# A fused attention and expert kernel: the first group of each attention program gets a PSUM bank for each of its four projections, and the value blocks are cleared behind the first moments

## What is computed

```python
x = x + L0_attention(layernorm(x), context)              # 16 heads of 8, no mask
x = x + L0_ffn(layernorm(x))                             # 8 experts pick 8 tokens each, attend, scatter back
# L1: three residual steps inside one block
x = x + L1_block(layernorm(x), context, mask_q, mask_k)  # self attention, cross attention, feed-forward of 512
x = x + L1_moe(layernorm(x))                             # 16 routed experts, 4 chosen, and 2 shared ones

def attention(xq, xkv, Wq, bq, Wk, bk, Wv, bv, Wo, bo, mask):
    q, k, v = xq @ Wq + bq, xkv @ Wk + bk, xkv @ Wv + bv
    scores = q @ k.T / sqrt(8)                           # per head
    return softmax(masked(scores)) @ v @ Wo + bo
```

## Time and profile before

| | |
|---|---|
| median of 3 runs | 2140.08 us (2134.15 to 2143.28) |
| time of the profiled execution | 2129.31 us |
| its span in the profile | 2127.5 us |
| TensorE busy | 1974.6 us, 93% |
| VectorE busy | 1629.4 us, 77% |
| ScalarE busy | 1063.6 us, 50% |
| GpSimd busy | 465.4 us, 22% |
| DMA over the span | 14 GB/s |
| granted TensorE clock, mean | 0.979 |
| first attention program | 0 to about 334 us |
| choice of tokens | about 334 to 591 us |
| second attention program | about 591 to 1295 us |
| late part | about 1295 us to the end |

### The profile page before, as it was taken

The page is one execution under the profiler, slowest core; times in us unless marked ns, Lnnn a source line. Parts: engine busy times, 40 slices in busy tenths (PEclk is TensorE's granted clock), DMA queues, the critical chain, the costliest instruction groups (busy, mean ns, idle before and its releaser), DMA issues. The chain is left out here.

```text
span 2127.5 us, 52756 instructions
## 1 busy us (share of the span) xinstructions
PE 1974.6 (93%) x19220; PEld 1530.4 (72%) x19220; DVE 1629.4 (77%) x4569; ACT 1063.6 (50%) x2180; POOL 465.4 (22%) x520
## 2 busy tenths in 40 slices
PE   7999995888869999999999998989999999999998
PEld 4666673677736666666666665767888888888887
DVE  5777775777538888888888884678888878888886
ACT  5656652666625555555455443544444444444442
POOL 1111111111002232323223223762111211111111
PEclk9999997999969999999999998999999999999999
DMA  3000000000000000001000002000000000000000
GB/s 128 31 30 20 30 10 1 1 1 1 1 20 2 0 0 0 0 1 32 20 30 30 20 10 68 1 1 6 6 6 5 10 6 5 6 6 10 6 5 11
DMA packets 27409, 30.50 MB, mean 14 GB/s; under 512 B 1952, under 2 KB 20640, under 8 KB 27040
## 3 DMA queue, kind: packets, MB, share of 16 engines
q1 hardware_dynamic: 27296, 29.18, 4.2%
HBM read 24.98 MB, written 4.19 MB: 14 GB/s over the span
## 5 line engine op out<-in xcount | busy, mean ns | idle before, releaser
L491 DVE TENSOR_REDUCE mx<-ps 128x8 f32<-128x512 f32 x384 | 261.9, 682 | 162.7 <-PE ps L681 162.5
L398 ACT ACTIVATE ex<-ps 128x512 f32<-128x512 f32 x384 | 230.2, 600 | 259.1 <-PE ps L699 257.0
L1125 ACT ACTIVATE y_res<-ps 128x512 f32<-128x512 f32 x288 | 172.4, 599 | 355.4 <-PE ps L1211 355.3
L1193 PEld LDWEIGHTS ps<-down,y_res 128*128 128x128 f32 x2048 | 267.2, 191 | 25.0 <-issue 3.0
L699 PE MATMUL ps<-pack,sh 128*128 128x128 f32 x1536 | 249.5, 284 | 29.7 <-DVE sh L493 28.8
L493 DVE TENSOR_TENSOR sh<-ps,mx 128x512 f32<-128x512 f32 x384 | 265.4, 691 | 13.2
L1193 PE MATMUL ps<-down,y_res 128*128 128x128 f32 x2048 | 270.7, 275 | 1.4 <-DVE y_res L1479 1.4
L1461 DVE TENSOR_TENSOR y_res<-ps,y_res 128x512 f32<-128x512 f32 x288 | 197.6, 686 | 80.4 <-PE ps L1211 66.0
L715 PEld LDWEIGHTS ps<-vblk,ex 128*64 128x64 f32 x6144 | 211.5, 138 | 65.0 <-issue 65.0
L699 PEld LDWEIGHTS ps<-pack,sh 128*128 128x128 f32 x1536 | 168.1, 141 | 121.2 <-issue 62.2
L715 PE MATMUL ps<-vblk,ex 128*64 128x32 f32 x6144 | 254.4, 226 | 0.0
(11 more groups left out here) (237 smaller groups left out, 3388.6 us busy)
## 6 DMA issues: line engine op xcount, KB each, us to landing
ctxT<-in_ctx SPq DMA_DIRECT2D x32, 256.0 KB, 2.8
x_res<-in_x SPq DMA_DIRECT2D x16, 256.0 KB, 2.8
kmi<-in_key_mask SPq DMA_DIRECT2D x16, 256.0 KB, 3.3
out<-y_res SPq DMA_DIRECT2D x16, 256.0 KB, 2.3
pack<-in_pack SPq DMA_DIRECT2D x1, 2053.0 KB, 10.2
wqkv<-in_wqkv SPq DMA_DIRECT2D x1, 1536.0 KB, 10.8
gate<-in_gate SPq DMA_DIRECT2D x6, 192.0 KB, 3.6
up<-in_up SPq DMA_DIRECT2D x6, 192.0 KB, 3.8
```

What stands on the lines that cost most here:

```text
L398: nc.scalar.activation(ex[:, u % 2], UB[u % 4].rearrange("p (c n) -> p c n", n=P), ACT.Exp).then_inc(e_ready, 1)
L491: nc.vector.tensor_reduce(mx[:, u % 2], sc, AX.X, ALU.max).then_inc(max_done, 1)
L1193: last = nc.tensor.matmul(YB[k % 2][:, t * D:(t + 1) * D], act_[:, k % 3, t * P:(t + 1) * P], down[:, k, :], start=True, stop=True)
```

## The change

It does three things. First, in the start of each attention program the rounds go to different banks: xT to `PREP`, k, q and v to the score banks `UB[0]`, `UB[1]` and `UB[2]`, which no one uses yet. TensorE then waits in the start only for the copy of xT (which q needs, and for a = 1 also k and v), no longer for the round before. Since `scores` of units 2 and 3 write `UB[2]`, TensorE waits there, in the first group, for all four copies. Second, in the second attention program VectorE takes the first moments ahead of the three memsets; in the first program the memsets stay where they were. ScalarE waits for the memsets only ahead of its first `copy_v`. Third, since q may now be copied by VectorE while k's copies run on ScalarE, the first q counts in a semaphore of its own, `first_q_copied`; ScalarE waits for it after k's copies and counts it on in `prep_copied`.

```diff
+        FIRST_BANK = {"xT": PREP, "k": UB[0], "q": UB[1], "v": UB[2]}
...
                     elif r == "k":
                         for j in range(HQ):
-                            spread_key(L, g, s, j)
+                            spread_key(L, g, s, j, FIRST_BANK[r])
                     elif r == "q":
                         if L.a == 0:
-                            copy_q(L, g, s)
+                            copy_q(L, g, s, FIRST_BANK[r])
                     else:
-                        copy_v(L, g, s)
+                        if L.a != 0:
+
+                            act.wait_ge(first_q_copied, 1)
+                            act.sem_inc(prep_copied, 1)
+                        act.wait_ge(vblk_set, 3)
+                        copy_v(L, g, s, FIRST_BANK[r])
...
-            act.wait_ge(vblk_set, 3)
             if a == 0:
                 act.wait_ge(consts_set, 3)
...
             def prep(g, s, L):
                 norm_stats(L, g, s)
                 key_mask_of_next(L, g, s)
-                copy_q(L, g, s)
+                if L.a != 0:
+                    clear_values()
+                copy_q(L, g, s, FIRST_BANK["q"], first_q_copied)
...
-                if n > 0:
+                bank = FIRST_BANK[what] if start else PREP
+                if start:
+                    if n > L.nr("xT"):
+                        pe.wait_ge(prep_copied, L.nr("xT") + 1)
+                elif n > 0:
                     pe.wait_ge(prep_copied, nth(g, NP, n - 1))
-                elif not start:
+                else:
                     pe.wait_ge(prep_copied, g * NP)
...
             def free_banks(g, u, first):
+                if first and u == 2:
+
+                    pe.wait_ge(prep_copied, NP)
```

More of the change, by code:

```diff
@@ L359, in copy_xT, with spread_key @@
                 nc.scalar.copy(srcT[:, :], PREP).then_inc(prep_copied, 1)
-            def spread_key(L, g, s, j):
+            def spread_key(L, g, s, j, bank=PREP):
                 if j == 0:
                     act.wait_ge(prep_ready, nth(g, NP, L.nr("k")))
-                last = nc.scalar.activation(kblk[:, s, :, j, :], by_batch(PREP), ACT.Identity, bias=L.bkm[:, j:j + 1],
+                last = nc.scalar.activation(kblk[:, s, :, j, :], by_batch(bank), ACT.Identity, bias=L.bkm[:, j:j + 1],
                                             scale=headmask[:, j:j + 1])
@@ L368, in spread_key, with copy_q, copy_v @@
                     last.then_inc(prep_copied, 1)
-            def copy_q(L, g, s):
+            def copy_q(L, g, s, bank=PREP):
                 act.wait_ge(prep_ready, nth(g, NP, L.nr("q")))
-                nc.scalar.activation(qd[:, s], PREP, ACT.Identity, bias=C["bqs"], scale=SCALE).then_inc(prep_copied, 1)
-            def copy_v(L, g, s):
+                nc.scalar.activation(qd[:, s], bank, ACT.Identity, bias=C["bqs"], scale=SCALE).then_inc(prep_copied, 1)
+            def copy_v(L, g, s, bank=PREP):
                 act.wait_ge(prep_ready, nth(g, NP, L.nr("v")))
@@ L381, in copy_v @@
                                 "p (t b) r e -> p b t r e", b=2)[:, b],
-                            PREP[64 * b:64 * b + 64, :].rearrange("p (t r j e) -> p j t r e", t=TILES, j=2, e=DH)[:, j])
+                            bank[64 * b:64 * b + 64, :].rearrange("p (t r j e) -> p j t r e", t=TILES, j=2, e=DH)[:, j])
                 last.then_inc(prep_copied, 1)
@@ L473, in key_mask_of_next, with copy_q @@
                                         ).then_inc(kmask_ready, 1)
-            def copy_q(L, g, s):
+            def copy_q(L, g, s, bank=PREP, copied=prep_copied):
                 if L.a == 0:
@@ L484, in copy_q @@
                     sc = qsc[:, s].unsqueeze(2).broadcast_to((P, GB, S))
-                nc.vector.scalar_tensor_tensor(by_batch(qd[:, s]), by_batch(PREP), L.bq, sc, ALU.add, ALU.mult
-                                               ).then_inc(prep_copied, 1)
+                nc.vector.scalar_tensor_tensor(by_batch(qd[:, s]), by_batch(bank), L.bq, sc, ALU.add, ALU.mult
+                                               ).then_inc(copied, 1)
             def shift(g, u):
@@ L573, in later_constants, with clear_values @@
                                             setup["any"][:, 2 + f:3 + f], None, ALU.mult).then_inc(qscale_diag, 1)
+            def clear_values():
+                nc.vector.memset(vblk[:, :, :, :, :], 0.0).then_inc(vblk_set, 1)
+                dve.wait_ge(vblk_set, 1)
+                nc.vector.memset(vblk[0:64, :, :, :, DH:DH + 1], 1.0).then_inc(vblk_set, 1)
+                nc.vector.memset(vblk[64:128, :, :, :, 16 + DH:17 + DH], 1.0).then_inc(vblk_set, 1)
             def prep(g, s, L):
@@ L641, in prep_slot @@
                     for t in range(TILES):
-                        last = nc.tensor.transpose(PREP[:, t * P:(t + 1) * P], xn[:, s, t, :], ident)
+                        last = nc.tensor.transpose(bank[:, t * P:(t + 1) * P], xn[:, s, t, :], ident)
                 elif what == "k":
@@ L645, in prep_slot @@
                         pe.wait_ge(c_loaded[s], loaded(L, g, s))
-                    last = nc.tensor.matmul(PREP, L.wk, source(L, s), start=True, stop=True)
+                    last = nc.tensor.matmul(bank, L.wk, source(L, s), start=True, stop=True)
                 elif what == "q":
-                    last = nc.tensor.matmul(PREP, L.wq, srcT[:, :], start=True, stop=True)
+                    last = nc.tensor.matmul(bank, L.wq, srcT[:, :], start=True, stop=True)
                 else:
                     for t in range(TILES):
-                        last = nc.tensor.matmul(PREP[:, t * D:(t + 1) * D], source(L, s)[:, t * P:(t + 1) * P], L.wv,
+                        last = nc.tensor.matmul(bank[:, t * D:(t + 1) * D], source(L, s)[:, t * P:(t + 1) * P], L.wv,
                                                 start=True, stop=True)
```

1 line of the change is left out of this document (added).

## The result

| | before | after |
|---|---|---|
| median | 2134.15 us (2129.23 to 2143.49, 15 runs) | 2127.27 us (2118.19 to 2132.79, 15 runs) |
| ratio | | 0.9958, 95% interval 0.9938 to 0.9977 |
| profiled execution, span | 2129.31 us, 2127.5 us | 2131.81 us, 2130.0 us |

The change is 0.42% faster, 9.0 us of 2134.15, with an interval of 4.9 to 13.2 us. The ratio is formed from all the runs; the two medians alone lie 6.9 us apart. More runs of the kernel before have moved its own median from the 2140.08 of the three shown first to 2134.15. The profiled execution after the change is 2.5 us *longer* than the one of before. A reader who compares just these two profiles would call the change a loss, so the first question is where in that profile the time was won and where it was lost.

A forecast was written before the change was run, and what follows sets the result against it. The prediction took the two serial program starts, where nothing hides the four rounds, as what counts: 7.12 us from the second plus 0.98 from the first, 8.1 us off 2140.1, gives 2132.0 us; range 2122 to 2139.

The forecast's parts named there:

- Moments ahead of the clearing: Second program's start: the moments, and the chain to q's matmul, come 4.16 us earlier, with the clearing hidden beside them.
- k behind q: Second program's start: k's matmul waits for xT's copy alone and follows q's matmul directly, 1.05 us gained.
- Scores behind k's copies: Second program's start: scores no longer wait behind v's matmul, 2.01 us gone, less 0.10 for passing on q's copy.
- First program, 0.98: First program's start: v's matmul comes right behind q's, and v and the scores move 0.98 us earlier.
- The clock, second start: Second program's start: early rise given back within the first pair, lasting rise as late as before, counted from the scores.
- The first rival: Clock rises early and stays, or returns a pair or two earlier: 7.4 us more gain, 2124.6 us; chance 0.31.
- The clock, first start: First program's start: q and v back to back for about 4 us may also bring the early clock; within the 0.31 rival.
- the third rival: Either start: a later clock rise pays back part, one pair more at half clock costing 3.5 us, 2135.5; chance 0.11.
- GpSimd held by the clearing: Second program's start: reciprocal waits for the memset's end, all behind it 3.4 us later, gain 4.7, 2135.4; chance 0.07.
- Slower: First groups: the clock stays down longer; two groups more would cost 28 us, 2160; chance 0.03.
- doesn't do what it says: Starts: another wait keeps k behind q or scores behind v, leaving only 4.16 us, 2135.9; chance 0.01.

The follow-up runs named there:

- the order alone: Kernel before, one bank kept, with only the moments moved in front of the clearing in the second program; ratio 0.9969 (0.9953 to 0.9985).
- the banks alone: Changed kernel, four banks kept, with the clearing back in front of the moments in both programs; ratio 0.9986 (0.9972 to 1.0).
- keeping the clock up: Changed kernel plus seven matmuls whose result no one reads in the second program's start; ratio to the kernel before 0.9922 (0.9900 to 0.9944).
- the memset in halves: Changed kernel with the big memset cut into two of 2048 elements; timed once, 2128.90 us.
- the clearing three times: Changed kernel with the big memset done three times in the second program; timed once, 2130.71 us.

## Why the prediction was right

The forecast was a gain of 8.1 us, 0.38%, within half a per cent; measured were 9.0 us, 0.42%. The absolute time is 4.7 us under the 2132.0 named, because the median it was taken from stood 5.9 us too high, and the two medians differ by 6.9 us and not by 8.1. The interval of 4.9 to 13.2 us doesn't tell 8.1 from 9.0, nor from the 9.6 that the starts add up to in this profile, so that the total came so close is in part luck. By its own steps:

- *Moments ahead of the clearing, 4.16.* Measured 5.05: by the first DMA issue the moments began at 5.09 before and at 0.04 now. The term was mis-sized. The 4.16 went from the memset's recorded start, and its first 0.80 us stood hidden in the 1.84 us of idle behind the barrier (0.95 now). The halves show that these 0.8 belong to the memset. The prediction had taken the 3.47 alone as its cost, and with it 0.85 ns an element, where the two together are 1.04. The Trainium skill ("VectorE: DVE Perf Modes", Zero memsets can be issued as uint32) gives a memset one cycle per element, and its Specifications give VectorE 0.96 GHz. An estimate from these is 4.27 us for 4096 elements, and the trace agrees: 0.80 + 3.47.
- *k behind q, 1.05.* 1.86 us from q to k where 1.87 was taken.
- *Scores behind k's copies.* From k's matmul to the first copy 1.88 us, not 2.11: the clock had risen just before. From the first copy to the scores 2.93, the 2.84 and 0.09 for the passing on, put at 0.10.
- Together 8.3 in place of 7.12 for the second start.
- *First program, 0.98.* 1.28 in this profile from q's matmul to the scores, since v ran into the full clock. Whether anything of it reaches the end depends on the clock (below).
- *The clock, second start.* It rose early and fell within the first pair, as forecast, and the lasting rise kept its distance of about 21 us to the first scores. The reason given for the fall is not shown. The prediction read the fall at 1285 to 1286 as one under small matmuls, with TensorE busy for all of that microsecond; the row just ahead (1283.76) stands behind 1.30 us of idle time, and this fall behind 2.08. Nothing here separates the small matmuls from the idle time. And of the pairs without a rise there were three, not the four that it counts: its fourth, at 635.20, is behind the rise. The first rival (a clock that stays, 7.4 us more) did not happen; with the clock kept up by force the three pairs took 7.1 us less, so the price was right.
- *The clock, first start.* What the prediction underrated is that an early rise can also be paid for: the third rival, at 0.11. It happened in the first start, and not in one execution alone. Each kernel below was profiled once:

| profile | first start | first scores | v of the second group |
|---|---|---|---|
| before | as before | 20.33 | 36.83 |
| the order alone | as before | 21.12 | 43.11 |
| after the change | changed | 19.47 | 39.02 |
| the banks alone | changed | 18.95 | 38.48 |
| keeping the clock up | changed | 19.19 | 38.99 |
| the memset in halves | changed | 19.50 | 39.23 |
| the clearing three times | changed | 19.81 | 36.30 |

  In the first four of the five with the changed start the clock came up at about 19, fell within 25 to 27 and returned within 35 to 37, and the second group is 1.65 to 2.4 us later than in the profile of before. In the fifth it came up at about 25.6 and stayed, and the gain of 0.5 us is kept. But the order of before has its scatter too: in the profile of the order alone TensorE's matmuls ran at half clock to about 41, and the second group is 6.3 us later. So no profile settles whether the first start's 0.98 is a gain on the average.
- *GpSimd held by the clearing* did not happen: the reciprocal took 1.01 us and xb 1.27, both partly beside the memset and as long as before (1.01 and 1.27). *Slower* and *doesn't do what it says* did not either.

That the local terms give 9.6 us together and the runs 9.0 leaves the clock's net share within the measurement's uncertainty, with no sign to it. The part that the experiments carry is the second start's.

## What to carry to other kernels

Work that nothing hides is found at the starts of programs, and a microsecond taken out there counts whole unless the clock takes it back, as it can have done in the first start here. Give each step of a start what it needs alone (its own buffer, its own wait), and put setup that is needed late behind the first chain. Look then at what the engines do in the first group behind it: here the half clock of TensorE in that group cost nearly as much as the start's waits, and a few unused matmuls, most of them in TensorE's idle time, gave it back. Compare two single profiles stretch by stretch from a common event, since the sum of one execution can point the other way than the change does.

## What was not expected of the hardware

A VectorE memset of 4096 float32 elements per partition shows 3.47 us busy and 0.80 us of idle ahead that belongs to it; with 2048 elements it is 1.76 and 0.38. The clock fell behind idle times of TensorE of 2.08 us (to 606.11), 1.19 us (to 24.96, ahead of the fall within 26 to 27) and 0.98 us (to 1260.35), while 0.99 us at the same place of the kernel before (to 1267.42) did not bring it down. It then stayed at half over 19 us in which TensorE was busy for 17.5 (607 to 626), and over 1265 to 1285, in which it was busy throughout: a busy share from the profile does not say that the clock will be full. And the same kernel scatters by 14.6 us from run to run, with mean granted clocks from 0.971 to 0.982.
